# A feed-forward stage on one core: when the second half's statistics are taken, when GpSimd takes its roots, and where the projection's first rows are written

## The reference

```python
def _layernorm(x, axis=-1, eps=1e-05):
    m = jnp.mean(x, axis=axis, keepdims=True)
    v = jnp.var(x, axis=axis, keepdims=True)
    return (x - m) / jnp.sqrt(v + eps)

def bitlinear(x, W, b):
    w_scale = jnp.clip(jnp.mean(jnp.abs(W)), EPS, None)
    Wq = jnp.clip(jnp.round(W / w_scale), -1.0, 1.0) * w_scale
    x_scale = jnp.clip(jnp.max(jnp.abs(x), axis=-1, keepdims=True), EPS, None)
    xq = jnp.clip(jnp.round(x * (QB / x_scale)), -QB - 1.0, QB) * (x_scale / QB)
    return jnp.einsum('bnd,hd->bnh', xq, Wq) + b

x = x + _L0_xattn_ref(_layernorm(x, axis=-1), ctx_768, ...)
# layer 0 feed-forward
h = bitlinear(_layernorm(x), W1, b1)          # 256 -> 1024
x = x + bitlinear(gelu(h), W2, b2)            # 1024 -> 256
# layer 1 attention: latents = _layernorm(x), normed once more
ln = layernorm(latents, ln_l_g, ln_l_b)
q, kv = ln @ Wq.T, ln @ Wlkv.T
...
```

## Time and profile before

| | us |
|---|---|
| runs | 922.33, 923.14, 924.48 |
| median | 923.14 |
| profiled execution | 925.02 |
| its span in the trace | 923.3 |
| mean granted clock of TensorE | 0.978 |

### The profile page before, as it was taken

One profiled execution on the slowest core, in us unless ns is written; L12 is line 12 of the kernel. 1 busy time (PEld: TensorE's weight loads), 2 busy tenths in 40 slices (PEclk: granted clock), 3 DMA queues, 4 the chain that ended last, 5 costly groups with the idle time before them and its releaser, 6 DMA issues.

```text
span 923.3 us, 15247 instructions
## 1 busy us (share of the span) xinstructions
PE 877.1 (95%) x4335; PEld 628.3 (68%) x4336; DVE 632.3 (68%) x1386; ACT 526.8 (57%) x834; POOL 400.1 (43%) x397
## 2 busy tenths in 40 slices
PE   8989989999999999999989999999999999999991
PEld 4646655545556656655557887878888888888881
DVE  6787968866567557656677789746666666666666
ACT  2567865546665775775545434326666666666650
POOL 2146655435776755765514556522222222222210
PEclk9988999989999999999999999999999999999997
DMA  9400000009478669559555100087811298526405
GB/s 296 104 0 1 1 1 1 1 4 347 190 284 331 226 271 366 221 234 396 201 220 222 52 1 1 12 335 325 316 36 34 80 346 340 206 96 246 119 5 183
DMA packets 49776, 153.58 MB, mean 166 GB/s; under 512 B 6255, under 2 KB 24427, under 8 KB 44101
## 3 DMA queue, kind: packets, MB, share of 16 engines
q1 hardware_dynamic: 45988, 143.75, 41.6%
q0 software_dynamic: 3744, 9.31, 3.2%
HBM read 97.34 MB, written 56.62 MB: 167 GB/s over the span
## 4 chain that ended last, share of the span: by engine, by line
PE 68%; DVE 13%; DMA 6%; ACT 4%; POOL 4%; issue 3%; SPq 1%; DVEq 0%; ACTq 0%; POOLq 0%
PE banks L1092 10%; PE banks L1343 8%; PE banks L1345 8%; PE banks L1344 8%; PE banks L1060 3%; PE banks L1084 3%; PE banks L1085 3%; DMA wsplit<-cv_hl 2%; PE banks L994 2%; PE banks L1381 2%; PE banks L1380 2%; PE banks L1382 2%; PE banks L1356 2%; POOL cv_hl L701 2%; DMA ring<-wsplit 2%
## 5 line engine op out<-in xcount | busy, mean ns | idle before, releaser
L1092 PE MATMUL banks<-wexp 128*65 128x512 f32 (+1 forms) x288 | 149.8, 601 | 2.5 <-ACT wexp L1654 2.5
L701 POOL TENSOR_TENSOR cv_hl<-wexp,cv_hl 128x1024 fp32r<-128x1024 f32 x45 | 108.7, 2422 | 51.7 <-ACT cv_hl L1631 51.1
L1343 PE MATMUL banks<-ring,x_hi 128*128 x312 | 127.4, 408 | 0.0
L1345 PE MATMUL banks<-ring,x_lo 128*128 x312 | 122.0, 391 | 0.0
L1344 PE MATMUL banks<-ring,x_hi 128*128 x312 | 121.8, 390 | 0.0
L1654 ACT ACTIVATE wexp<-banks 128x512 f32<-128x512 f32 x128 | 75.9, 597 | 47.6 <-PE banks L1085 47.5
L1790 ACT ACTIVATE banks<-wexp 128x1024 f32 x72 | 73.5, 1020 | 47.7 <-DVE aux L2550 47.7
L1768 ACT ACTIVATE aux<-banks 128x512 f32<-128x512 f32 x78 | 46.6, 598 | 61.2 <-PE banks L1345 45.3
L1084 PE MATMUL banks<-q_hi,k_hl 128*128 128x512 f32 x144 | 77.2, 536 | 1.7 <-ACT q_lo L1622 1.0
L2148 DVE TENSOR_REDUCE neg_ab<-banks 128x1 bf16<-128x736 f32 x64 | 59.3, 927 | 23.7 <-PE banks L1060 20.1
L1345 PEld LDWEIGHTS banks<-ring,x_lo 128*128 128x128 f32 x312 | 58.6, 188 | 13.1
(11 more groups left out here) (387 smaller groups left out, 2239.9 us busy)
## 6 DMA issues: line engine op xcount, KB each, us to landing
wsplit<-cv_hl SPq DMA_DIRECT2D x45, 1024.0 KB, 8.0
ring<-wsplit SPq DMA_DIRECT2D x32, 1280.0 KB
wexp<-in_L_ffn_w SPq DMA_DIRECT2D x40, 512.0 KB, 5.9
wexp<-in_expert_biases SPq DMA_DIRECT2D x8, 1152.0 KB, 6.6
ring<-wsplit SPq DMA_DIRECT2D x4, 1024.0 KB, 9.6
wexp<-moe_y SPq DMA_DIRECT2D x7, 512.0 KB, 6.3
wexp<-in_L_ffn_sw SPq DMA_DIRECT2D x5, 512.0 KB, 9.0
x_sb<-in_x SPq DMA_DIRECT2D x4, 512.0 KB, 9.5
```

What stands on the lines that cost most here:

```text
L701: g.tensor_tensor(sides(hl[:, PIECE:2 * PIECE]), raw, sides(hl[:, 0:PIECE]).bitcast(f32), ALU.subtract).then_inc(s['cv_lo'], 1)
L1092: mm(pb[5 + half][0:DA, :], vh[b][0:w, c, :], pT[q % 3][0:w, :], start=c == 0, stop=c == len(KTILES) - 1).then_inc(s['a_pv'], 1)
L1343: mm(o[:], x_hi[u][:, kc, :], hi, start=kc == 0 and not primed, stop=False, skip_group_check=primed)
L1345: last = mm(o[:], x_lo[u][:, kc, :], hi, start=False, stop=primed and kc == KC - 1, skip_group_check=primed)
```

## The change

1. DVE's statistics of tiles 8 to 15 are split: two between turns -3 and -2, two between -2 and -1, four with the aggregation between -1 and 0.
2. POOL's root for these tiles moves from tiles 4 to 7 (ahead of their rows) to tiles 6 and 7: the first guess ahead of tile 6's rows, one refinement behind tile 6's work, two behind tile 7's.
3. POOL's root for the projection's rows 0 to 7 begins in tile 14, goes on in tile 15 ahead of its parts, and has its last two refinements behind them.
4. DVE writes the projection's first two row tiles inside turn 12, ahead of keeping tile 15's turned rows, into places 2 and 3 of xn (the places now are (t + 2) % 4); the next two follow in `between(12)`.
5. PE's bias of tile 15 moves from turn 13 to between the first two `proj_in`.
6. The constants k_hl and k_hi are set at the program's start instead of after the root.

```diff
@@ GpSimd, start @@
-            g.memset(bias_b[:], 0.0)
+            link(g.memset(bias_b[:], 0.0))
+            for u in range(2):
+                link(g.memset(k_hl[u][:, S + SK:KW].bitcast(f32), 0.0))
+                link(g.memset(k_hi[u][DH:DA, 0:S + SK].bitcast(f32), 1.0))
@@ GpSimd, tiles @@
             for t in range(T):
-                if t == TB - 4:
+                if t == TB - 2:
                     pool.wait_ge(s['f_rstd'], 2)
                     root_first(TB, T)
-                if TB - 4 < t < TB:
-                    root_turn(TB, T, rstd if t == TB - 1 else root_s)
...
                 g.tensor_tensor(x_sb[:, t, :], x_sb[:, t, :], b2_all[:], ALU.add).then_inc(s['f_pool'], 1)
+                if t == TB - 2:
+                    root_turn(TB, T, root_s)
+                if t == TB - 1:
+                    for to in (root_s, rstd):
+                        root_turn(TB, T, to)
+                if t == T - 2:
+                    root_first(0, LN_EARLY)
+                if t == T - 1:
+                    root_turn(0, LN_EARLY, root_s)
             pool.wait_ge(s['f_byx'], T)
             bias_parts(T - 1)
-
-            root_first(0, LN_EARLY)
-            for k in range(3):
-                root_turn(0, LN_EARLY, ln_r if k == 2 else root_s)
+            for to in (root_s, ln_r):
+                root_turn(0, LN_EARLY, to)
             pool.sem_inc(s['f_pool'], 1)
@@ TensorE @@
             def ffn_turn(i):
-                if there(i + 2):
+                if there(i + 2) and i + 2 != T - 1:
                     ffn_bias(i + 2)
...
                 if i == T - 4:
                     pe.wait_ge(s['f_rows'], T)
                     proj_in(0)
+                    ffn_bias(T - 1)
                     proj_in(1)
@@ VectorE @@
                     link(statistics(i - 1))
+                if i == T - 4:
+                    ve.wait_ge(s['f_pool'], T + 1)
+                    for t in range(2):
+                        proj_tokens(t)
...
             def between(i):
+                if i == -3:
+                    attended_stats(2, 0, 2)
+                if i == -2:
+                    attended_stats(2, 2, 4)
+                if i == -1:
+                    attended_stats(3)
+                    aggregate(TB, T)
+                    v.tensor_scalar(root_a[:, TB:T], mv[:, TB:T, 1], LN_EPS, None, ALU.add).then_inc(s['f_rstd'], 1)
...
                 if i == T - 4:
-                    ve.wait_ge(s['f_pool'], T + 1)
-                    ve.wait_ge(s['f_xqT_full'], T)
-                    for t in range(4):
+                    for t in range(2, 4):
                         proj_tokens(t)
...
-            ffn_turn(-3)
-            attended_stats(2)
-            attended_stats(3)
-            aggregate(TB, T)
-            v.tensor_scalar(root_a[:, TB:T], mv[:, TB:T, 1], LN_EPS, None, ALU.add).then_inc(s['f_rstd'], 1)
             ve.wait_ge(s['ld_ffn'], NLD['ld_ffn'])
-            ffn_turns(ffn_turn, between, first=-2)
+            ffn_turns(ffn_turn, between, first=-3)
```

More of the change, by code:

```diff
@@ L648, in _ @@
                 g.tensor_tensor(x_sb[:, t, :], x_sb[:, t, :], b2_all[:], ALU.add).then_inc(s['f_pool'], 1)
+                if t == TB - 2:
[7 more added lines that the diff above has]
+                    root_turn(0, LN_EARLY, root_s)
             pool.wait_ge(s['f_byx'], T)
             bias_parts(T - 1)
-            root_first(0, LN_EARLY)
-            for k in range(3):
-                root_turn(0, LN_EARLY, ln_r if k == 2 else root_s)
+            for to in (root_s, ln_r):
+                root_turn(0, LN_EARLY, to)
             pool.sem_inc(s['f_pool'], 1)
             for u in range(2):
-                link(g.memset(k_hl[u][:, S + SK:KW].bitcast(f32), 0.0))
-                link(g.memset(k_hi[u][DH:DA, 0:S + SK].bitcast(f32), 1.0))
                 link(g.memset(vh[u][:, :, DH:DA], 1.0))
@@ L983, in proj_in @@
                 for kc in range(KC):
-                    last = tr(pb[7][:, kc * P:(kc + 1) * P], xn[:, t % 4, kc * P:(kc + 1) * P], ident[:])
+                    last = tr(pb[7][:, kc * P:(kc + 1) * P], xn[:, (t + 2) % 4, kc * P:(kc + 1) * P], ident[:])
                 last.then_inc(s['l_xT_full'], 1)
@@ L1965, in attended, with attended_stats @@
                 link(last)
-            def attended_stats(it):
-                for u in range(4):
+            def attended_stats(it, u0=0, u1=4):
+                for u in range(u0, u1):
                     t = it * 4 + u
@@ L2065, in proj_tokens @@
                     ve.wait_ge(s['l_xT_full'], t - 3)
-                v.tensor_scalar(xn[:, t % 4, :], x_sb[:, t, :], mv[:, t, 0:1], ln_r[:, t:t + 1], ALU.subtract, ALU.mult).then_inc(s['l_xh'], 1)
+                v.tensor_scalar(xn[:, (t + 2) % 4, :], x_sb[:, t, :], mv[:, t, 0:1], ln_r[:, t:t + 1], ALU.subtract, ALU.mult).then_inc(s['l_xh'], 1)
             def proj_squares(t):
```

## The result

The changed kernel takes 916.92 us, the median of four runs (915.82, 916.12, 917.72, 920.41), against 923.20 for the kernel before run beside it: ratio 0.994, 95% interval 0.9917 to 0.9962, so 6.3 us or 0.6% faster. Two more sets of runs of the same kernel in the experiments gave 0.9914 (0.9886 to 0.9941) and 0.9918 (0.9903 to 0.9933). All 16 runs have a median of 915.9, the 59 runs of before beside all sets one of 923.1: 7.2 us. (A 60th, of 1255.29 us at a mean clock of 0.648, is a slow run and left out.)

The account below looks back on a forecast made before the run. TensorE, busy 95% of the span, was taken as the bound, so savings count only where it waits or runs at half clock. 4.6 - 0.3 + 4.2 - 0.3 = 8.2 us, median 923.14 to 914.9; range 912.5 to 918.3.

Parts of the forecast that it names:

- Statistics over three turns: Feed-forward stage's start: splitting DVE's eight statistics brings the fifth hidden-row maximum earlier; 4.6 us booked.
- the start that moved: Stage's start: 2.1 us of the 4.6 from the earlier first maximum; the other 2.5 from the clock not falling.
- The likeliest case: The forecast itself, 60%: clock at 1.00 from 62 to 78 us at the stage's start; own range 912.8 to 916.6.
- the clock falls all the same: Rival, 25%: clock low at the stage's start as long as before, only 2.1 us won there; median 917.4.
- GpSimd's roots: Tiles 7 and 8: refinements delay GpSimd's rows of tile 8, making PE late once; -0.3 us, bounds 0 and 1.1.
- The last turns: Stage's end: earlier root, two row tiles and bias bring tile 13's output 4.2 us earlier, less 0.3 for the memset.
- The clock: Stage's end: 1.33 us from the first projection at full clock, 0.2 from two turns at full clock.
- Bias: Stage's end: tile 15's bias fits into PE's wait between the first two row tiles; 0.72 us.
- Contention with the memset: Stage's end: DVE's two row tiles meet GpSimd's 1.09 us memset, making the turned rows late by 0 to 0.9; -0.3 us.
- the wait of 1.94: Stage's end: PE's wait for DVE's first projection row tile after tile 15 disappears; 1.94 us of the 4.2.
- the second rival: Last turns, 7%: DVE waits for GpSimd's last root ahead of tile 15, costing 1.5 to 2 us more; 916.7.
- Memsets at the start: Program's start: GpSimd's four memsets, at most 2.2 us, fit its idle time before its first wait; 0 us.

Follow-up runs that it names:

- the control: Changed kernel plus one register operation per expert turn on PE and ACT, holding the waited-on register to at least 2; 915.7 us, 0.9914; run again 915.3, 0.9918.
- the filled kernel before: Kernel before with matrix products nobody reads in PE's waits at the feed-forward stage's start (three, ten, one); 920.7 us, ratio 0.9967.
- the head alone: Kernel before with only the stage-start edits (statistics over three turns, GpSimd's roots in tiles 6 and 7); 920.0 us, ratio 0.9964.
- the tail's edits alone: Kernel before with only the stage-end edits (projection root, two row tiles in turn 12, tile 15's bias, constants at the start); 920.0 us, ratio 0.9958.
- the statistics as 4, 2, 2: Changed kernel with the eight statistics shared out over the three turns as four, two, two instead of two, two, four; 916.2 us, ratio 0.9926.
- four filled traces: Unread products in PE's waits: kernel before 920.7 us; changed kernel 916.5; kernel before with stage-end edits 914.6; changed kernel with refinement and memset moved 915.6.

## Why the prediction was right, and where it wasn't

The time, 916.9, lies in the range and 2.0 us above the forecast of 914.9; over all 16 runs, 915.9, it is 1.0 above. The steps one by one:

**Statistics over three turns (4.6 forecast): the sum held where the clock did, but what it was put down to was wrong.** Between the traces that have it as forecast (clock lost before, kept after) the gain is 27.86 - 22.90 = 4.96 us, and the turns after were laid out well: 3.9, 5.7, 3.9 and 3.9 us were forecast, 4.08, 5.37, 3.80 and 3.91 measured in the control. But the prediction divided the 4.6 into "2.1 us are the start that moved; 2.5 us rest on the clock", and this step failed. With the clock held in both, the kernel before takes 23.27 and the changed one 22.90: the move itself is worth 0.37 us, the clock up to 4.6. The intervals tell why. From a first maximum at 5.74 us behind the last sums the control has the four above; the filled kernel before has 3.80, 3.91, 3.82, 3.89 from one at 7.85. The 2.1 us won at the start are given back, 1.74 of them, in the two turns that now hold the statistics, since DVE sets the pace there (PE waits 1.24 us for it in tile 3). I had that in my own sum (5.7 for the third interval) and still booked the start as a gain of its own, comparing it with turns of before that were long because of the clock.

**The kernel before was taken to be what its one trace showed.** Its low stretch was 13.6 us there and 6.8 in the next trace, which had the head at 25.52. The gain against that one is 2.6 us. The change's own trace had a fall too: 27.86 - 25.20 = 2.66. So the head's gain is 5.0, 2.6 or near 0.3 (25.52 - 25.20), by what the clock does in either; the head alone gave 3.3 in the medians. The likeliest case (no fall) held in five of seven traces of the split statistics. That it held in as many of the untraced executions is not shown.

**The rival "the clock falls all the same"** had 25% and 917.4. It is what the profiled execution did: 10.2 us low, with no wait longer than 0.87 us ahead of it. Its price was right (2.66 where I said 2.1) for a reason that wasn't. Against traces without a fall it cost 4.59 us in before (27.86 - 23.27) and 2.30 here (25.20 - 22.90); the difference, 2.29, with the 0.37 of the move gives the 2.66. A fall shorter by 3.4 us makes up about half of the 2.29, at the 0.34 us per us low of before (an estimate, 4.59/13.6); the rest fits that DVE's long turn lay inside the low stretch, where DVE waited 1.54 us for PE, and is not shown apart.

**GpSimd's roots (-0.3, bounds 0 and 1.1):** -0.15 us, by the sixth interval with and without. It queues the parts of the bias factor behind the refinements, which is shown by moving one of them. No run shows the 0.2 to 0.3 us that were forecast: PE took up tile 8 already 0.14 us behind the end of the parts (85.22 to 85.36), and lost 0.15 in all.

**The last turns (+4.2 and -0.3):** 4.11 in the first trace, 4.31 in the tail's edits alone, which are without the roots' cost; forecast were 3.9. The terms could be measured one by one. The clock (1.33 in the projection and 0.2 in the turns): 1.51, as 48.93 - 47.57 = 1.36 and 0.15 for the roots that the second of these kernels has in addition. Bias 0.72: 0.75. Contention with the memset -0.3: -0.11, the one term that was mis-sized, as PE could spare more than the 0.3 us I gave it. What is left at full clock, 47.57 - 44.78 - 0.75 + 0.11 = 2.15, stands against the wait of 1.94. The clock's term too is one that some executions have (3.4, 3.4 and 6.8 us low in three traces, none in a fourth of the old end). The wait for GpSimd's root, the second rival, didn't come: L633 ended at 119.78, before DVE's statistic at 119.95, though its margin was only 0.2 us. Of the memset's contention with the row tiles the rule drawn from the Trainium skill's "SBUF — State Buffer", "Who interferes with whom", is borne out in kind, not in full: two row tiles take 1.45 us beside the memset and 0.74 without. They end 0.15 us behind it, where a wait to its end and a whole row tile (0.37) would end 0.37 behind.

**Memsets at the start (0):** the four took 2.8 us (6.53 to 9.36) of POOL's idle time; the last sums started at 57.13 in the first trace and at 56.08 and 56.44 in the controls, before at 56.67 and 56.25. No cost shows.

**What fell short** of the forecast are 1.0 us over the 16 runs and 2.0 in the four of the result. For the four, the profiled one lost 0.46 us in the first DMA and 1.71 behind the stage, which the change doesn't touch. For the 16, the likely part is that before loses less on average than in its first trace. The mean granted clock on record for each run covers the whole execution and tells no stretch, but it points that way. The 55 runs of before that have one average 0.9794, 38 us at half clock, against 0.9777 and 41 us in the first trace: 3 us less, which at 0.34 us each is 1 us (an estimate). The changed kernel's 16 average 0.985, no lower than its two traces without a fall (0.984 and 0.985), and only the profiled run of the result has 0.981. How often the clock falls with the split statistics stays open all the same, and what decides it between two executions of one program too: two of seven traces is no rate, and nothing on record shows the cause.

## What to carry to other kernels

Where an engine's work is spread out to shorten a wait, ask what the same turns would take at full clock in both versions: work that the bounding engine has to do anyway gives back what the earlier start won, and here only 0.4 of 5 us was the spreading (1.0 with the statistics as 4, 2, 2). If the rest is the clock, cheap products in the wait may hold it too: in all four filled traces it stayed up in the head, which is few to build on. A single trace says neither that a fall always comes nor how long it lasts: take two or three of each kernel. Cut the traces at marks of the program and compare stretches; that told 0.15 us where medians of ten runs told 1.5. When two costs are removed at once, put a mark between them: of the 0.27 us that the tail won, the sixth interval shows 0.15 to be the roots'.

## What the runs showed of the hardware

The same program with like waits of PE (0.87 or 0.65, then 0.52 us) was granted 0.50 for 10.2 us from 64.4 us on in one execution and 1.00 throughout 56 to 80 us in two others. Over the three stretches of 2 us from 58 us on PE was busy 1.16, 1.78 and 1.48 us in the first and 1.13, 1.48 and 1.84 in the control, so nothing there tells them apart. Around a wait of 2.75 us the clock fell in all three traces, for 13.6, 6.8 and 13.6 us; with that wait filled down to 0.58 us by products that nobody reads it did not fall there in either of two traces. Behind 1.94 (in one 1.97) and 0.99 us at the old end it fell in three of four. A low stretch of 3.4 us beside a bound on DVE cost nothing (22.92 against 22.90, where PE's wait for DVE in tile 3 shrank from 1.00 to 0.33 us), one of 13.6 us cost 4.6.

Two row tiles on DVE (128x256 f32 each) took 1.45 us beside a memset of 64x1024 f32 on GpSimd and 0.74 us without it.
